# Context rows turned by TensorE instead of by VectorE, SP and DMA, with a new order of steps

## The reference

```python
x = x + local_attn(layernorm(x))            # softmax over keys with |j - i| <= 3, with biases
x = x + cross_attn(layernorm(x), ctx_1024)  # keys and values from the 120 context rows, with biases
z = layernorm(x)                            # then the ffn block works on z and adds to it:
z = z + causal_attn(rmsnorm(z) * n1) ;  z = z + moe(rmsnorm(z) * n2)
x = x + z
# moe: gate = softmax(z @ gate_w.T); up 256 -> 1024, silu, down 1024 -> 256,
# scaled by the normalised sum of the two largest gate values
```

## Time and profile before

| what | value |
|---|---|
| median of 3 runs | 3476.36 us (3472.11 to 3479.12) |
| profiled execution | 3476.82 us, its span 3475.1 us |
| TensorE (PE) busy | 3419.0 us, 98% of the span |
| VectorE (DVE) busy | 2707.3 us, 78% |
| GpSimd (POOL) busy | 2498.0 us, 72% |
| ScalarE (ACT) busy | 1781.6 us, 51% |
| mean granted clock of TensorE | 0.999 |
| DMA | 239.16 MB, 20.8% of 16 engines' time on the main queue |

### The profile page before, as it was taken

The page is one execution under the profiler, slowest core; times in us unless marked ns, Lnnn a source line. Parts: engine busy times, 40 slices in busy tenths (PEclk is TensorE's granted clock), DMA queues, the critical chain, the costliest instruction groups (busy, mean ns, idle before and its releaser), DMA issues.

```text
span 3475.1 us, 93089 instructions
## 1 busy us (share of the span) xinstructions
PE 3419.0 (98%) x36137; PEld 2751.0 (79%) x36137; DVE 2707.3 (78%) x5941; ACT 1781.6 (51%) x4177; POOL 2498.0 (72%) x3160
## 2 busy tenths in 40 slices
PE   7899999999999999999999999999999999999998
PEld 5577888888788888888888888888888888888876
DVE  5778788787787787787787787787787787787763
ACT  3354554555555555555555555555555555555542
POOL 5877777777777777777777777777777777777732
PEclk9999999999999999999999999999999999999999
DMA  6112122122122122122222222222122122121200
GB/s 198 50 55 83 52 74 83 52 75 81 54 75 71 63 76 71 62 76 68 65 76 66 67 76 64 70 76 68 65 76 68 63 79 64 66 80 61 68 5 10
DMA packets 194610, 239.16 MB, mean 69 GB/s; under 512 B 115783, under 2 KB 161155, under 8 KB 177795
## 3 DMA queue, kind: packets, MB, share of 16 engines
q1 hardware_dynamic: 194178, 233.20, 20.8%
HBM read 172.78 MB, written 58.26 MB: 66 GB/s over the span
## 4 chain that ended last, share of the span: by engine, by line
PE 92%; DVE 3%; SPq 2%; DMA 1%; ACT 1%; issue 1%; POOL 1%; DVEq 0%; ACTq 0%; POOLq 0%
PE ps L1016 13%; PE ps L1025 13%; PE ps L894 11%; PE ps L994 10%; PE ps L943 9%; PE ps L872 9%; PE ps L928 8%; PE ps L966 8%; PE ps L900 4%; PE ps L852 3%; PE ps L922 1%; SPq L760 1%; PE ps L980 1%; PE ps L832 1%; DVE max_blocks L1458 1%
## 5 line engine op out<-in xcount | busy, mean ns | idle before, releaser
L666 POOL TENSOR_TENSOR chunks<-v_windows,xT 128x560 f32<-128x560 f32 (+1 forms) x384 | 877.6, 2305 | 160.2 <-DVE xT L1433 156.8
L1135 ACT ACTIVATE prob<-ps 128x256 f32<-128x256 f32 (+2 forms) x1536 | 676.9, 544 | 444.1 <-PE ps L943 444.1
L1458 DVE TENSOR_REDUCE max_blocks<-ps 128x4 f32<-128x480 f32 (+2 forms) x1280 | 769.2, 668 | 38.0 <-PE ps L928 35.4
L661 POOL TENSOR_TENSOR chunks<-rest,k_windows 128x512 f32<-128x512 f32 (+1 forms) x384 | 555.2, 1454 | 299.3 <-DVE rest L1399 277.2
L1016 PE MATMUL ps<-xT,w_up 128*128 128x256 f32 x2048 | 487.0, 386 | 2.7 <-ACT xT L1088 2.7
L1025 PE MATMUL ps<-w_down,held 128*128 128x256 f32 x2048 | 459.1, 382 | 1.0 <-DVE held L1514 1.0
L1016 PEld LDWEIGHTS ps<-xT,w_up 128*128 128x128 f32 x2048 | 378.2, 190 | 91.9 <-ACT xT L1088 23.9
L1025 PEld LDWEIGHTS ps<-w_down,held 128*128 128x128 f32 x2048 | 383.8, 190 | 72.2 <-issue 20.2
L1292 POOL TENSOR_SCALAR_AFFINE_SELECT prob<-prob 128x512 f32<-128x512 f32 x512 | 310.7, 640 | 138.2 <-ACT prob L1135 138.0
L1412 DVE TENSOR_REDUCE held<-chunks 128x80 f32<-128x560 f32 (+1 forms) x384 | 292.8, 763 | 90.9 <-POOL chunks L666 90.8
L1412 DVE TENSOR_REDUCE xT<-chunks 128x32 f32<-128x512 f32 (+1 forms) x384 | 294.1, 766 | 67.7 <-POOL chunks L661 67.4
(11 more groups left out here) (150 smaller groups left out, 6789.1 us busy)
## 6 DMA issues: line engine op xcount, KB each, us to landing
k_windows<-passed_on SPq DMA_DIRECT2D x64, 1024.0 KB, 4.9
v_windows<-passed_on SPq DMA_DIRECT2D x64, 1024.0 KB, 5.0
x<-in_x SPq DMA_DIRECT2D x64, 256.0 KB, 2.9
passed_on<-rest SPq DMA_DIRECT2D x64, 256.0 KB, 3.7
passed_on<-held SPq DMA_DIRECT2D x64, 256.0 KB, 3.7
held<-nmaxT SPq DMA_DIRECT2D x1024, 2.0 KB
out<-x SPq DMA_DIRECT2D x64, 256.0 KB, 2.2
y<-in_ctx SPq DMA_DIRECT2D x64, 120.0 KB, 2.8
```

What stands on the lines that cost most here:

```text
L661: return engine.tensor_tensor(chunk_of(c).rearrange("p (j d) -> p j d", d=D), token_rows["q"][s][:, b, :].unsqueeze(1).to_broadcast([P, n, ...
L666: return engine.tensor_tensor(chunk_of(c).rearrange("p (h i j) -> p h i j", i=HD, j=WINDOW), window("v", b * D + first * HD, (HD, n), (1, ...
L1135: last = nc.scalar.activation(prob_pair(seq, L, m)[0:keys, :, r, col:col + qs], of_pair, ACT.Exp, scale=SCALE)
L1458: nc.vector.tensor_reduce(of_heads[:, ms[0]:ms[-1] + 1, :, r], src, AX_X, ALU.max, negate=True).then_inc(emptied[b], 1)
```

## The change

`BY_DMA` becomes empty. So flip, spread and gather of the context fall away, and the step turn_ctx takes their place: two transposes by TensorE into one bank and a copy by ScalarE. The memsets that padded the context rows for the flip go as well. The planner's cost for one DMA issue of the step place rises from 0.42 to 0.56 us, and its landing time falls from 1.6 to 1.45 us; two constants that only the DMA way uses change too. POSITION and SHIFTED are replaced as a whole, which gives another order on all engines. In the cut below, the rest of SHIFTED is left out.

```diff
--- before.py
+++ after.py
@@ -68,15 +68,15 @@
 
 Part = namedtuple("Part", "name args engine busy lag after takes gives kb", defaults=(0,))
 LAG = {"SP": 1.1, "PE": 0.21, "ACT": 0.2, "DVE": 0.2, "POOL": 0.1}
-DMA_ISSUE = 0.42
+DMA_ISSUE, PLACE_ISSUE = 0.42, 0.56
 PLACES = {"lane": LANES, "prob": PROBS, "k_window": 1, "v_window": 1, "chunks": 1}
 
 DIVIDED = {"max": "rows", "scores": "rows", "values": "columns", "gate": "columns"}
 DIVIDE, REJOIN, CHANGE = 0.1, 0.22, 0.15
 WIRE = 330.0
 LANDING = 1.1
-BY_DMA = ("ctx",)
-FLIP, SPREAD_KB = 0.56, 1000
+BY_DMA = ()
+FLIP, SPREAD_KB = 0.6, 450
 COOLS_AFTER, WARMS_IN = 1.5, 3.4
 EMPTIED = 0.24
 
...
-POSITION = {("turn", (0,)): 0.5152, ("project_rows", ("k",)): 0.6146, ("project_rows", ("v",)): 0.8394,
-    ("project_rows", ("q",)): 0.9724, ("project", (1, "k")): 1.5434, ("turn_out", ()): 1.9724, ("project_out",
-    (0,)): 1.9726, ("turn", (1,)): 2.0916, ("project", (1, "q")): 2.2114, ("max", (1, 0)): 2.2942, ("max", (1, 1)):
-    2.3582, ("project", (1, "v")): 2.5156, ("scores", (1, 1)): 2.7414, ("scores", (1, 0)): 2.9953, ("values", (1,)):
-    3.0525, ("project_out", (1,)): 3.1003, ("turn", (2,)): 3.2781, ("project", (2, "q")): 3.3391, ("project", (2,
-    "k")): 3.515, ("max", (2, 0)): 3.7297, ("max", (2, 1)): 3.9164, ("max", (2, 2)): 3.9235, ("scores", (2, 1)):
-    4.0853, ("scores", (2, 0)): 4.2209, ("scores", (2, 2)): 4.2938, ("project", (2, "v")): 4.3395, ("values", (2,)):
-    4.3627, ("project_out", (2,)): 4.7637, ("turn", (3,)): 4.9846, ("up", (0,)): 4.9981, ("up", (1,)): 5.0088,
-    ("gate", ()): 5.0851, ("up", (2,)): 5.0914, ("up", (3,)): 5.2026, ("down", ()): 5.2779}
+POSITION = {("turn_ctx", ()): -0.1461, ("turn", (0,)): -0.105, ("project_rows", ("k",)): 0.0183, ("project_rows",
+    ("v",)): 0.0345, ("project_rows", ("q",)): 0.1413, ("project", (1, "v")): 0.7715, ("project", (1, "k")): 0.8873,
+    ("turn_out", ()): 1.0488, ("project_out", (0,)): 1.0917, ("turn", (1,)): 1.3378, ("project", (1, "q")): 1.3667,
+    ("max", (1, 0)): 1.7909, ("max", (1, 1)): 1.8716, ("scores", (1, 1)): 2.0244, ("scores", (1, 0)): 2.0798,
+    ("values", (1,)): 2.2493, ("project_out", (1,)): 2.4457, ("turn", (2,)): 2.7713, ("project", (2, "q")): 2.8102,
+    ("project", (2, "k")): 2.9958, ("max", (2, 0)): 3.0239, ("max", (2, 1)): 3.0812, ("max", (2, 2)): 3.1837,
+    ("scores", (2, 1)): 3.4898, ("scores", (2, 0)): 3.5548, ("scores", (2, 2)): 3.7905, ("project", (2, "v")):
+    3.8011, ("values", (2,)): 3.8718, ("project_out", (2,)): 4.0395, ("turn", (3,)): 4.1835, ("gate", ()): 4.2195,
+    ("up", (2,)): 4.2502, ("up", (0,)): 4.2504, ("up", (3,)): 4.2506, ("up", (1,)): 4.3526, ("down", ()): 4.7094}
...
-SHIFTED = {("fetch", ("v",), "SP"): -0.1399, ("gate", (), "DVE"): -0.788, ("gather", ("ctx",), "SP"): -1.0217,
-    ("max", (1, 0), "DVE"): -0.5461, ("max", (2, 0), "DVE"): 0.3503, ("max", (2, 1), "DVE"): -0.0364, ("max", (2,
-    2), "DVE"): -0.3119, ("moments", (0,), "DVE"): -0.0061, ("moments", (0,), "POOL"): -0.4538, ("moments", (1,),
...
+SHIFTED = {("down", (), "DVE"): 0.0922, ("fetch", ("v",), "SP"): 0.2583, ("load", (), "SP"): -0.4273, ("max", (1,
+    0), "DVE"): -0.0714, ("max", (1, 1), "DVE"): -0.0061, ("max", (2, 0), "DVE"): -1.1956, ("max", (2, 1), "DVE"):
+    -0.0215, ("moments", (0,), "DVE"): -1.1092, ("moments", (0,), "POOL"): -0.4703, ("moments", (1,), "DVE"):
...
@@ -244,7 +243,7 @@
                 a = part(*step, "PE", pe, operands, [("quad", step)])
                 last = [part(*step, "DVE", 2.28 if layer == CROSS else 2.4, [a, *last], (), [("quad", step)])]
             a = part("shift", (layer,), "DVE", 0.2, last)
-            shifted = part("place", (layer,), "SP", 8 * DMA_ISSUE, [a], lag=1.6)
+            shifted = part("place", (layer,), "SP", 8 * PLACE_ISSUE, [a], lag=1.45)
             ready = []
             held = []
             for u, unit in enumerate(score_units(layer)):
@@ -1308,8 +1307,6 @@
             def _(dve):
                 nc.vector.memset(neg_half[:], -0.5)
                 nc.vector.memset(neg_one[:], -1.0)
-                for s in range(LANES):
-                    nc.vector.memset(cx[s][3 * SLOT:P, :], 0.0)
                 nc.vector.memset(zero_rows, 0.0).then_inc(filled_ones, 1)
                 for s in range(LANES):
 
```

More of the change, by code:

```diff
@@ L97 @@
-SHIFTED = {("fetch", ("v",), "SP"): -0.1399, ("gate", (), "DVE"): -0.788, ("gather", ("ctx",), "SP"): -1.0217,
-    ("max", (1, 0), "DVE"): -0.5461, ("max", (2, 0), "DVE"): 0.3503, ("max", (2, 1), "DVE"): -0.0364, ("max", (2,
-    2), "DVE"): -0.3119, ("moments", (0,), "DVE"): -0.0061, ("moments", (0,), "POOL"): -0.4538, ("moments", (1,),
[L100 to L108, removed]
-    "ACT"): 0.0846, ("scores", (2, 2), "POOL"): 0.0556, ("send", ("k",), "SP"): 0.2136, ("send", ("v",), "SP"):
-    0.0853, ("shift", (2,), "DVE"): 0.0419, ("spread", ("ctx",), "SP"): 0.4639, ("store", (), "SP"): 0.1334,
-    ("turn", (0,), "ACT"): -0.1168, ("turn", (2,), "ACT"): -0.1938, ("turn", (3,), "ACT"): 0.023, ("turn_out", (),
-    "ACT"): 0.2366, ("up", (0,), "ACT"): -0.1485, ("up", (1,), "ACT"): 0.4134, ("up", (1,), "DVE"): -1.6074, ("up",
-    (2,), "ACT"): -0.0256, ("up", (2,), "DVE"): -0.2456, ("up", (3,), "ACT"): 0.0327, ("up", (3,), "DVE"): 0.2719,
-    ("weigh", (), "POOL"): -0.4291, ("window_exp", (), "ACT"): 0.1431, ("window_reduce", (0,), "DVE"): 0.1855,
-    ("window_reduce", (1,), "DVE"): 0.0471, ("window_reduce", (2,), "DVE"): -0.1832, ("window_reduce", (3,), "DVE"):
-    -0.6162, ("window_reduce", (4,), "DVE"): -1.0845, ("window_reduce", (5,), "DVE"): -1.038, ("window_reduce",
-    (6,), "DVE"): 0.0786, ("window_reduce", (7,), "DVE"): -0.377, ("window_reduce", (9,), "DVE"): 0.0386,
-    ("window_reduce", (10,), "DVE"): -0.0649, ("window_reduce", (11,), "DVE"): 0.6853, ("window_sum", (), "DVE"):
-    0.7557, ("window_times", (0,), "POOL"): -0.3458, ("window_times", (1,), "POOL"): 0.0182, ("window_times", (2,),
[L120 to L123, removed]
```

23 lines of the change are left out of this document (added).

## The result

| what | before | after |
|---|---|---|
| median, on one chip | 3476.4 us | 3497.62 us (3495.72 to 3500.76) |
| profiled execution, its span | 3476.82, 3475.1 us | 3495.72, 3493.9 us |
| TensorE busy | 3419.0 us | 3435.2 us |
| VectorE, ScalarE, GpSimd busy | 2707.3, 1781.6, 2498.0 us | 2680.6, 1830.8, 2498.1 us |
| DMA | 239.16 MB | 223.40 MB |

A forecast was written before the change was run, and what follows sets the result against it. TensorE's own sequence of steps was taken to bound the kernel. From 3476.8 us, +14.1 for the transposes, -26.9 for one excursion into strips less and +3 for the placing gave 3467.0 us, range 3444 to 3500.

The forecast's parts named there:

- The turn: Two added TensorE transposes of context rows per sequence cost 0.22 us, +14.1 us in all; ScalarE's copy stays hidden.
- rival D: The added transposes don't overlap, each holding TensorE 0.27 us: 35 us for the turn, time 3488; chance 0.02.
- Flip, spread and gather: Removing the context's DMA way frees VectorE and SP's queue, not TensorE's path: priced at nothing.
- One excursion less: TensorE goes into array strips six times per period instead of seven, each 0.42 us: -26.9 us in all.
- The place chain: Cross layer, max (1, 1) to scores (1, 1) through VectorE and DMA: cover shrinks to 9.10 us, 0.05 us wait, +3 us.
- The cover of the second placing: From max (2, 2) to scores (2, 1): five full steps and others, over 12 us for a chain of about 9.
- The turns of layer 3 and layer 0: Layer 3 keeps 1.3 us of slack; layer 0 has one full step (1.72 us) for its copy; nothing added.
- The bank wait of project_rows k: About 0.2 us of waiting in this step before strips stays; if it goes, another -13 us.
- Filling and draining: The start and end of the run, outside the steady periods: priced at nothing, within 10 us either way.
- rival C: Slower: the cross layer's placing leads, TensorE waits 0.4 to 0.8 us per period, 3490 to 3515 us; chance 0.26.
- Rival B: No change that can be told: new small waits at shorter covers add 6 to 19 us, 3470 to 3483; chance 0.25.

The follow-up runs named there:

- e3: The kernel before with only the context rows turned by TensorE (turn_ctx at 0.5153), old order otherwise: 3505.8 us, 1.0086.
- e2: The changed kernel with its new order, but the context rows by VectorE, SP and DMA again: 3507.17 us, 1.0091.
- e8: The changed kernel with gate behind values 1, context by DMA and three of four GpSimd masks left out before values 2 (output differs): 3482.14 us, 1.0019.
- e1: The changed kernel with one position moved, so that TensorE runs gate after values 1 instead of before: 3477.11 us, 1.0004.
- e5: The changed kernel with five more, long satisfied waits on TensorE in front of values 1: 3508.61 us, 1.0095.
- e10: The changed kernel, gate first, without TensorE's waits that others imply (for placed maxima and for banks of values 1): 3476.61 us, 1.0.
- e9: e1 without TensorE's waits that others imply (for placed maxima and for banks of values 1): ratio 1.0002.
- e13: e9 with VectorE's addition for layer 1's output cut to 128 of 512 columns (output differs): 3467.35 us, 0.9976.
- e16: e9 with project_out of layer 1 one step sooner in TensorE's order, so project q stands between it and scores (2, 1): 3578.79 us, 1.0293.
- e6: e1 with five more, long satisfied waits on TensorE in front of values 1: 3479.2 us, 1.001.

## Why the prediction was wrong

1. **The turn, +0.22 us.** Right in size: 0.30 to the next step in after, with the 0.09 of going into strips, and 0.21 between full steps in e3. e2 and e8 add what I didn't see: in the new order values 2 would have waited for GpSimd's masks in that time anyway. The Trainium skill (TensorE: Matmul & The Clock Gate, PE-mode transpose), named under rival D, gives some 275 ns for a full 128 x 128 transpose in one kernel's context. The duration here agrees (275 ns, mean of 128), but a duration is no price: two of them take 0.30 us to the next step. The group of after by shape:

```profile
L858 PE MATMUL ps<-ident,y 120*128 120x120 f32 x128 | 24.7, 275 | 3.2 <-DMA y<-in_ctx 2.7
```

2. **Flip, spread and gather, nothing.** Right in the steady part. The DMA way costs 8.5 us in the head in the new order (e2), the other way is worse by 14.6 in the old (e3).
3. **One excursion less, -0.42 us: here it failed.** The order is the one that I sorted, and the entries and exits of the six excursions cost what they had cost. But two excursions were not worth what they had been. The step that failed is "After has six: ... again two with a change inside", which priced [values 1, gate, scores (2, 1)] and [max (2, 2), gate, values 1] alike. In the one, gate has 1.75 us of computing in front, during which its successor's waits are worked through: the two semaphore instructions of scores (2, 1) start 0.41 and 0.30 us before gate's first matmul (1764.92 in the kernel before). In the other, the first semaphore instruction of values 1 starts 0.02 us after gate's first matmul, gate itself is the cover of all five, and it is too short: +0.33 us, 64 times, some 21 us. That is as much as the whole slowdown; e1, e5 and e10 each show it. The second part is the pair of scores: inner groups at 0.51 instead of 0.43, +0.15 us, some 9.6 us. The term took two excursions into one at the old price of the groups, and scores (2, 0) then had to wait for the bank that VectorE's addition after project_out 1 empties (e9 and e13).
4. **The place chain, +0.05 us.** Right, the chain is covered: 1.2 us of waits in all. The cover of the second placing has six full steps and not the five that I counted, so it is longer still. The turns of layer 3 and layer 0 had the slack that I worked out.
5. **The bank wait of project_rows k.** It halved, 2.04 to 1.93. The 0.10 us that project (1, v) takes more are no wait: it now stands in front of strips, and this is one of the six entries in the sum.
6. **Filling and draining, nothing.** -3.1 and +5.6 us: inside my 10 us. 2.2 of the 5.6 lie between the last turn of layer 3 and down (12.74 us in e1 instead of 10.54, with a wait of 1.49 for VectorE); the other 3.4 are located in the drain and not explained.

The time lies in the window of rival C, but C's mechanism did not occur. Rival B had the right kind, "new small waits of 0.1 to 0.3 us", and half the size, since I took one such place and there were two. With the two terms the sum is 3467 + 21 + 9.6 = 3497.6, the 3497.62 that was measured. That it fits so closely is luck: the 3 us of the placing did not come and the bank wait gave 6 us back, and small steps and the tail cost about as much. e13, which has neither of the two terms, has a period of 52.087 us; the measured 52.254 of the kernel before less the priced 0.15 is 52.10.

## What to carry to other kernels

When an order is priced by the old distances of its steps, ask of each short step what stands behind it in the queue, and count that step's waits, satisfied ones too: here they are free behind 1.17 us of computing and cost their full time behind a step of 0.2 us. When the profile lists no wait, look at the sequencer's own rows before calling a distance a price. And when a step moves to the place directly in front of another, ask whether they share a bank (e13, e16). Thin out the waits that others imply before tuning an order, since then the order may be chosen for other reasons (e10). And a part that fills another wait, as the turn does here, can't be judged by itself: each part alone is slower than both together (e2, e3).

## What the runs showed of the hardware

Satisfied semaphore waits on TensorE's queue have a price when a short step stands in front, here one of 16 short matmuls: 0.106 us for each EVENT_SEMAPHORE, which holds up to two waits. With two of them gate to values 1 is 0.25 us (e10), with five 0.56 (the changed kernel), with seven 0.77 (e5). Behind the 1.17 us of max (2, 2) neither two, five nor seven cost anything (e9, e1, e6). The Trainium skill (Perfetto Trace Analysis, Sequencer-only Instruction) says that of such an instruction the profile holds the execution alone, not the fetch, decode and semaphore wait; the trace agrees, since each is recorded with 51 ns while one starts every 106.

A wait for a bank that comes late need not be in the list of waits either. TensorE's semaphore instruction for bank 2 starts 0.04 us after VectorE's addition ended, in every one of 53 sequences, and the strips around it run at 0.51 us a group instead of 0.43 (e9 and e13), yet no idle time of TensorE is listed there.
